# Moving the output projection of one token tile behind the projections of the next tile in a hand-ordered block kernel

## What is computed

```python
def ffn(x):                      # x is layer-normed, x_prev is x one token earlier
    xr = mu_r * x + (1 - mu_r) * x_prev
    xk = mu_k * x + (1 - mu_k) * x_prev
    r = sigmoid(xr @ W_r.T); k = xk @ W_k.T
    return r * (relu(k)**2 @ W_v.T)
def attn(x):
    k = mix_k(x) @ Wk.T; v = mix_v(x) @ Wv.T; r = sigmoid(mix_r(x) @ Wr.T)
    # per head, over time: num = sa + exp(u+k) v ; den = sb + sum exp(u+k)
    #                      sa = ew*sa + exp(k) v ; sb = ew*sb + sum exp(k)
    return (r * num/den) @ Wo.T
x = x + 0.5*ffn(layernorm(x)); x = x + attn(layernorm(x)); x = x + 0.5*ffn(layernorm(x))
```

## Time and profile before

| | us |
|---|---|
| median of 3 runs (3678.76 to 3795.9) | 3679.82 |
| the profiled execution, its own time | 3679.53 |
| its span on the slowest core | 3678.0 |
| spans of the eight cores | 3673.4 to 3678.0 |
| TensorE busy | 1810.1 (49%) |
| VectorE busy | 1568.4 (43%) |
| ScalarE busy | 764.4 (21%) |
| mean granted TensorE clock | 0.718 of full |

### The profile page before, as it was taken

The page is one execution under the profiler, slowest core; times in us unless marked ns, Lnnn a source line. Parts: engine busy times, 40 slices in busy tenths (PEclk is TensorE's granted clock), DMA queues, the critical chain, the costliest instruction groups (busy, mean ns, idle before and its releaser), DMA issues.

```text
span 3678.0 us, 25100 instructions; the slowest of 8 cores (3673.4 to 3678.0 us)
## 1 busy us (share of the span) xinstructions
PE 1810.1 (49%) x7192; PEld 777.0 (21%) x7192; DVE 1568.4 (43%) x3754; ACT 764.4 (21%) x1222; POOL 6.5 (0%) x11
## 2 busy tenths in 40 slices
PE   1454545544554545455445545454454545454554
PEld 0222212221222212222222212122221222121222
DVE  1444444444444444444444444444434444444443
ACT  1221221222222222212212122221122211222211
POOL 0000000000000000000000000000000000000000
PEclk9767777777776777767777777777677767777776
DMA  9000000000000000000000000000000000000000
GB/s 163 16 12 12 0 12 12 12 12 12 1 12 12 12 12 0 12 12 12 12 6 6 12 12 12 12 0 12 12 12 12 3 9 12 12 12 12 0 6 12
DMA packets 18212, 49.97 MB, mean 14 GB/s; under 512 B 2593, under 2 KB 2722, under 8 KB 18082
## 3 DMA queue, kind: packets, MB, share of 16 engines
q0 software_dynamic: 7280, 14.68, 2.6%
q1 hardware_dynamic: 6194, 16.92, 1.4%
q10 hardware_dynamic: 4608, 16.78, 1.1%
HBM read 46.27 MB, written 16.78 MB: 17 GB/s over the span
## 4 chain that ended last, share of the span: by engine, by line
PE 48%; DVE 23%; ACT 13%; issue 9%; DVEq 3%; another core or an unknown queue 1%; ACTq 1%; DMA 0%; SPq 0%
PE p L366 21%; PE p L368 19%; PE p L309 4%; DVE xr L342 3%; PE p L493 3%; PE p L490 2%; DVE s1F L253 2%; ACT junk L246 2%; DVE dbuf L337 2%; DVE xk L342 2%; ACT zfF L320 2%; ACT ka_fm L417 2%; DVE z_tmF L286 1%; DVE Aprime L514 1%; DVE numb L511 1%
## 5 line engine op out<-in xcount | busy, mean ns | idle before, releaser
L366 PE MATMUL p<-fwvt_s,ka_fm 128*128 128x512 bf16 x512 | 275.8, 539 | 300.1 <-ACT ka_fm L417 300.1
L366 PE MATMUL p<-fwrt_s,xr 128*128 128x512 bf16 x512 | 268.4, 524 | 313.4 <-DVE xr L342 313.4
L309 PE MATMUL p<-idb_s,z_tmF 128*128 128x128 bf16 x512 | 64.8, 307 | 608.5 <-DVE z_tmF L286 608.5
L368 PE MATMUL p<-fwvt_s,ka_fm 128*128 128x512 bf16 x512 | 269.5, 526 | 0.0
L368 PE MATMUL p<-fwrt_s,xr 128*128 128x512 bf16 x512 | 261.7, 511 | 0.0
L366 PE MATMUL p<-fwkt_s,xk 128*128 128x512 bf16 x512 | 193.8, 379 | 92.0 <-ACT esig L387 92.0
L423 DVE TENSOR_TENSOR u_sb<-recbF,p 128x512 f32<-128x512 f32 x64 | 44.0, 687 | 424.9 <-PE p L368 424.9
L366 PE MATMUL p<-wkt_s,xk 128*128 128x512 bf16 x256 | 137.6, 537 | 159.7 <-DVE xk L342 159.7
L368 PE MATMUL p<-fwkt_s,xk 128*128 128x512 bf16 x512 | 193.9, 379 | 0.0
L309 PEld LDWEIGHTS p<-idb_s,z_tmF 128*128 128x128 bf16 x512 | 49.6, 139 | 638.0 <-issue 638.0
L246 ACT ACTIVATE junk<-R 128x1024 bf16<-128x1024 f32 x96 | 100.9, 1051 | 394.4 <-DVE R L426 355.3
(11 more groups left out here) (114 smaller groups left out, 3161.4 us busy)
## 6 DMA issues: line engine op xcount, KB each, us to landing
R<-x SPq DMA_DIRECT2D x32, 512.0 KB, 3.3
out<-R ACTq DMA_DIRECT2D x32, 512.0 KB, 2.7
fwrt_s<-fwrt POOLq DMA_DIRECT2D x1, 2048.0 KB, 20.4
fwkt_s<-fwkt POOLq DMA_DIRECT2D x1, 2048.0 KB, 38.0
fwvt_s<-fwvt POOLq DMA_DIRECT2D x1, 2048.0 KB, 50.7
wkt_s<-wkt POOLq DMA_DIRECT2D x1, 2048.0 KB, 62.2
wvt_s<-wvt POOLq DMA_DIRECT2D x1, 2048.0 KB, 74.7
wrt_s<-wrt POOLq DMA_DIRECT2D x1, 2048.0 KB, 86.3
```

Source lines behind the costliest of these rows:

```text
L309: last = t.transpose(p0bank[:, cc * 128:(cc + 1) * 128], src[:, cc * 128:(cc + 1) * 128], idb[:])
L366: t.matmul(pa[:], lhsbuf[:, cc * 128:(cc + 1) * 128], wv[:, cc, 0:512], start=st, stop=sp)
L368: last = t.matmul(pb[:], lhsbuf[:, cc * 128:(cc + 1) * 128], wv[:, cc, 512:1024], start=st, stop=sp)
```

## The change

In the loop, the call of `attn_d(i)` is moved behind the call of `attn_a(i+1)`. Nothing else changes: the same instructions run with the same waits on data, but on each of the three engines the instructions of `attn_d(i)` stand behind those of `attn_a(i+1)`. It concerns the 31 passes with a tile i+1.

```diff
@@ -578,10 +578,10 @@
             if i + 1 < n_tiles:
                 rF1[i + 1] = ffn_b(i + 1, Rb[(i + 1) % 3], *st_f1[i + 1],
                                    nslot="A")
-            rA = attn_d(i, Rb[i % 3], evg)
             if i + 1 < n_tiles:
                 st_a[i + 1] = attn_a(i + 1, Rb[(i + 1) % 3],
                                      r_ev=rF1[i + 1], s1_ev=None)
+            rA = attn_d(i, Rb[i % 3], evg)
             st_f2 = ffn_a(i, Rb[i % 3], "F2", r_ev=rA, s1_ev=None)
             rF2 = ffn_b(i, Rb[i % 3], *st_f2, nslot="F2")
             store(i, rF2)
```

## The result

The changed kernel takes 3824.48 us (median of 10 runs) against 3679.56 for the kernel before, beside it. The ratio is 1.0393 with a 95% interval of 1.037 to 1.0416: slower by 145 us, or 4.67 us for each of the 31 passes. The forecast was slower by 200 us, 6.48 us a pass, with a range that began at 3840.

A forecast was written before the change was run, and what follows sets the result against it. The prediction took a chain hopping between TensorE, VectorE and ScalarE as the bound. Loss 9.28 less gain 2.80 is 6.48 us a tile, times 31 = 200.9 us, giving 3880 us, 5.5% slower; range 3840 to 3930.

The forecast's parts named there:

- Place 1: Ahead of A's layer norm: its sum `s1A` no longer waits for `wot` and starts 2.80 us earlier a tile.
- Start of `wot`: After `wrt`: copy `gfm` queues behind `recbA` on ScalarE, so `wot` starts 5.74 us after `wrt` ends.
- From `wot` to F2's transposes: Ahead of F2's norm: sums, `junk` and whole norm take 7.33 us from `wot`'s end, read off the last tile.
- `wot`, 6.15 us: Output projection behind the new gap: starts at the low clock and takes 6.15 us, against 3.62 at full clock.
- The rest about as today: All other work: stays about as it was while `wot` runs slow; the main forecast, 85%.
- 40 us on each side: Range: two slow-starting projections differing from their mean in the same direction make 40 us on each side.
- the clock is given back elsewhere: Rival: other slow-starting projections run at 2.4 GHz, saving 2.0 us each; in part, within 2%: 3%; in full, faster: 2%.
- a mean that moves by more than 30 ns: Sign of a wrong prediction: projections the change doesn't touch change their mean matmul times by more than 30 ns.
- The direction: Whole kernel: slower 95%, same 3%, faster 2%, with about 2% as the limit for no change.
- the two places: Ahead of A's layer norm, gain 2.80 us a tile; between `wrt` and F2's layer norm, loss 9.28 us.

The follow-up runs named there:

- e1: Kernel before, with only VectorE's two sums of the output projection into `R` moved behind A's layer norm; 3596.94 us, ratio 0.9753.
- e6: The order of e1 with unused filler matmuls ahead of TensorE's waits, as in e3; 3247.24 us, ratio 0.8812 in the third set.
- e2: Kernel before, with only `wot` and its sums moved behind `attn_a(i+1)`; transposes of `g2` and copy `gfm` stay; 3680.59 us, ratio 0.9993.
- e5: Changed kernel plus 21 unused filler matmuls, only between the transposes of `g2` and `wot`; 3808.23 us, ratio 1.0289.
- e10: Kernel before plus extra VectorE products in F2's residual path; two products: 3683.71 us, ratio 0.9996; four: 3781.41 us, ratio 1.0256.
- e4: Changed kernel plus unused filler matmuls ahead of TensorE's waits, including 21 ahead of `wot`; 3453.38 us, ratio 0.9366.
- e3: Kernel before plus unused filler matmuls ahead of TensorE's waits, its order kept; 3342.16 us, ratio 0.9064.

## Why the prediction was wrong

- **Place 1, gain 2.80 us:** right. 11.51 to 8.71 us in the trace after; 83 us for it alone in e1, 90 with the clock held in e6.
- **Start of `wot`, 5.74 us after `wrt`:** right, 5.72, and e2 shows the cause: with the copy out of ScalarE's queue the wait is 1.43 and the loss gone.
- **From `wot` to F2's transposes, 7.33 us:** right, 7.34.
- **`wot`, 6.15 us:** mis-sized. It is 5.52 in the mean, made of two values, 4.9 to 5.1 and 6.5. I took it from two single rows, 6.06 and 6.25, where single starts differ by up to 1.6 us; the 5.6 us that the prediction itself worked out from the mean of `fwvt` was the better value. This term makes 20 us.
- **"The rest about as today":** this is the step that failed. The prediction treated the slow starts of the other projections as constants that may scatter, and gave the scatter 40 us on each side. They are not constants. A shift of a few us in one place changes how long the clock stays low in the others, and here they gave back 1.13 us a tile, 35 us. With the 20 us of `wot` that is 55 of the 56 us that are missing. e5 and e10 show this response in isolation: 59 us saved became 16, and 47 us added became 4 or 5. The rival "the clock is given back elsewhere" was this mechanism, but I priced it only as whole projections turned fast, and so gave it 5%. The prediction's own sign for this, a mean that moves by more than 30 ns, was too coarse: `fwvt` moved by 28 ns, the most of all, and on 32 matmuls a tile that is already 0.74 us of busy time.
- **The direction, 95% slower:** right. The order costs 3.6 us a tile with the clock held (e4 against e3), and 4.1 with `wot` alone held (e5 against the kernel before).

What stays open: what sets the size of a step (3.4 us here), and why in e1 and e5 two neighbouring tiles share one. No run changed what the steps depend on other than by taking the low clock away.

## What to carry to other kernels

Before a stage is moved behind another, look at all of its instructions on all engines: here the matmuls could move for nothing, and a 1 us copy queued behind a ln and an exp on ScalarE was what opened the gap; while the cheap half of the move, one sum on VectorE taken out of the way of a layer norm, was worth 83 us by itself. In a loop whose TensorE falls to its low clock several times a pass, don't trust a sum of gains and losses of 1 or 2 us: here 0.36 us a tile gained at the two places brought nothing (e2), 1.52 added cost 0.15 and 3.05 added cost 3.3 (e10), while 2.80 gained brought 2.7 (e1). The range must span a step of the pass on either side. Hold the clock with filler matmuls when two orders are to be compared.

## What was not expected of the hardware

A delay of 1.52 us a tile on the chain cost 4 or 5 us in 3680, and one of 3.05 us cost 102. The tile periods of the settled loop were 109.1 to 109.6 (most tiles of e1), 112.2 to 113.0 (before, e2, nearly all of e10 with two products), 115.6 to 116.8 (the changed kernel, e10 with four, most tiles of e5) and 119.1 to 119.7 (the changed kernel); the tiles of e1 and e5 in between lie on these values in pairs. Only with the clock held near 0.97 did the short delay cost most of its length. And nearly a tenth of the kernel, 337 us, went away when TensorE's waits were filled with matmuls that nobody reads, at a mean granted clock of 0.97 instead of 0.72.
